# A recurrent attention cell behind two convolutions: its input product folded into the q, k and v weights, its convolutions on 32x32 tiles, its splits and stacks image by image

## The chip, the core and the metric

The kernel runs on one core of a Trainium2 chip. The core has TensorE (PE, matrix products; its weight loads are listed apart as PEld), VectorE (DVE), ScalarE (ACT), GpSimd (POOL) and SyncE (SP, which here only issues transfers). The engines run their own instruction streams in order and wait for each other by semaphores. The metric is the device time of one execution in microseconds.

## What is computed

Four layers follow each other on x of shape 4 x 32 x 32 x 32, each x + layer(gn(x)), where gn normalises every channel of every image: a second-order Volterra convolution (L0), a 3x3 convolution (L1), an attention cell (L2) and a Hartley transform layer (L3). The change is in L2, of which with a zero state only one attention of four has to be computed in full:

```python
xin = jnp.einsum('nchw,oc->nohw', x, W_in) + b_in[None, :, None, None]
h = jnp.zeros_like(xin)
pairs = ((xin, xin), (xin, h), (h, xin), (h, h))
for idx, (query, token) in enumerate(pairs):
    q = _conv(query, Wq[idx], 'SAME').reshape(n, HEADS, HC, -1)
    k = _conv(token, Wk[idx], 'VALID').reshape(n, HEADS, HC, -1)
    v = _conv(token, Wv[idx], 'VALID').reshape(n, HEADS, HC, -1)
    w = jax.nn.softmax(jnp.einsum('nhcq,nhcd->nhqd', q, k), axis=-1)
    a = jnp.einsum('nhcd,nhqd->nhcq', v, w).reshape(n, CA, hh, ww)
...
i, g, o = sigmoid(pre[0]), tanh(pre[2]), sigmoid(pre[3])
hout = o * jnp.tanh(i * g)
return jnp.einsum('nchw,oc->nohw', hout, W_out) + b_out[None, :, None, None]
```

There are 4 images of 4 heads of 8 channels, 1024 queries and 900 keys.

## The kernel before

All 4 images x 32 channels lie on the 128 partitions. The order of every engine's work is written out by hand. Line numbers are those of the profile.

L0 ends at L1007 and L1 runs from L1040 to L1060. Between the two PE multiplies zeros (`keep_clock`, L990), 3 + 4 + 13 times, until the second normalisation (DVE, L718) is there; then L1052 spreads the image over three row shifts. The third normalisation ends L1.

L2 then begins with the input product on PE (L1072, 24 products), added to its bias by ACT and DVE into a padded, three-fold copy `xst` (L631, L776). The convolutions for k, q and v follow (`conv`, L1084), each with 96 input rows (three row shifts of 32 channels) against 32 outputs. Between them stand three small products for the mean over the keys that the third attention needs (L1096, L1102, L1109). v is transposed by seven transposes and four products (L1115, L1120). k is split for all images at once into three bf16 parts (high, middle, low) and a difference of its two halves (`diff`), q likewise by halves of the image: ACT copies (L635 to L649), DVE subtracts (L793 to L822). SP writes each part to HBM (L508, L511) and reads it back three-fold, "stacked", into 72 rows (`stack_k` L519, `stack_q` L527), first two heads of k, then the q of image 0, then the rest of image 0 and 1.

The attention's order comes from `attention_plan` (L132). Half s is one half of an image's queries. For each of 16 groups of 128 queries PE makes two "max blocks" of 450 keys (L1137): a `diff` block, of which ACT takes the relu (L670), and a `first` block, to which DVE adds the relu and takes the maximum over keys (L870). I call them a pair. Blocks 0 to 31 are the 16 pairs of half 0. Then DVE splits the maxima (L847 to L854), PE turns them (item 32, L1149), DVE copies and POOL issues a transfer that puts them below the queries (L595). Blocks 33 to 45 belong to half 1. Then the first score tile comes (L1169), which ACT exponentiates (L662), and from there on scores, value products (L1187) and max blocks are woven together to the end of the last half. The PSUM bank of a block is taken from a ring of 7 banks for the first 41 items (`prologue`), then from a ring of 3, and PE waits until the bank's last block was read. After each of these first blocks PE multiplies zeros once, 256 columns.

## Time and profile before

| | us |
|---|---|
| median of 3 runs | 320.7 (318.45 to 322.28) |
| the profiled execution | 321.3 |
| its span, first to last instruction | 319.5 |
| PE busy | 291.6 |
| DVE busy | 209.0 |
| ACT busy | 183.5 |
| POOL busy | 30.2 |

The mean granted clock of TensorE was 0.994 of full speed. A busy PE means that a product was under way, not that the array was full. Times in the rows count from the start of the span; the profiled execution is 1.8 us longer than its span.

### The profile page before, as it was taken

What the parts mean: (1) busy time and instruction counts of PE and PEld (TensorE: products, weight loads), DVE (VectorE), ACT (ScalarE), POOL (GpSimd) and SP (SyncE); (2) the same over time, 40 slices, a digit from 0 to 9 for tenths busy, and PEclk for the clock granted to TensorE, in tenths of its full rate; (3) what the DMA queues carried; (4) which work ended last, traced back from release to release, by engine and by line L of the source; (5) the groups of instructions that cost most, each with busy time, mean ns of one, the idle gap of its engine ahead of it and who ended that gap; (6) DMA issues with size and microseconds to landing.
All of it is one profiled execution on the core that took longest, in us unless ns stands there. A gap on an engine that the chain in (4) does not pass through costs nothing.

```text
span 319.5 us, 10019 instructions
## 1 busy us (share of the span) xinstructions
PE 291.6 (91%) x4308; PEld 130.8 (41%) x4316; DVE 209.0 (65%) x483; ACT 183.5 (57%) x346; POOL 30.2 (9%) x34
## 2 busy tenths in 40 slices
PE   5999999798998999999999999999999899877774
PEld 2686634233455334333333333343333232334751
DVE  5980272577368647886977888879788122477664
ACT  1102011116246898897988888878888898313700
POOL 6400000010000000100100101001010010800000
PEclk9999999999999999999999999999999999999799
DMA  7100000003671483794000000000000000000001
GB/s 224 72 4 4 4 12 0 2 0 89 198 139 32 105 141 88 185 330 167 1 2 4 3 4 2 2 5 3 4 2 2 2 3 2 0 2 3 2 4 66
DMA packets 3819, 15.28 MB, mean 48 GB/s; under 512 B 807, under 2 KB 1623, under 8 KB 3359
## 3 DMA queue, kind: packets, MB, share of 16 engines
q1 hardware_dynamic: 3519, 14.54, 16.6%
q8 instruction: 34, 0.56, 0.8%
q0 software_dynamic: 256, 0.11, 0.2%
q14 instruction: 10, 0.08, 0.1%
HBM read 12.17 MB, written 2.37 MB: 45 GB/s over the span
## 4 chain that ended last, share of the span: by engine, by line
PE 41%; DVE 12%; issue 5%; ACT 5%; DMA 2%; ACTq 0%; DVEq 0%
PE ps L1187 11%; PE ps L1137 10%; PE ps L1169 10%; PE ps L1307 3%; ACT arena_b L662 3%; DVE sums L870 3%; DVE mx L875 3%; PE ps L1193 2%; PE ps L1252 2%; DMA arena_a<-mt_sb 2%; ACT arena_a L691 1%; PE ps L1328 1%; DVE arena_b L965 1%; DVE arena_a L940 1%; PE ps L1260 1%
## 5 line engine op out<-in xcount | busy, mean ns | idle before, releaser
L662 ACT ACTIVATE arena_b<-ps 128x512 f32<-128x512 f32 x232 | 126.3, 616 | 20.8 <-PE ps L1169 19.6
L1137 PE MATMUL ps<-arena_a 72*32 72x450 bf16 (+1 forms) x889 | 88.5, 355 | 3.0 <-DVE mx L870 1.5
L1169 PE MATMUL ps<-arena_a 75*32 75x512 bf16 x896 | 85.1, 380 | 0.8 <-DMA arena_a<-mt_sb 0.5
L875 DVE TENSOR_REDUCE mx<-ps 128x1 f32<-128x450 f32 x120 | 68.7, 618 | 3.6 <-PE ps L1137 3.5
L870 DVE CUSTOM_DVE_ANT_0 sums<-ps,relus 128x450 bf16<-128x450 f32 x68 | 42.1, 625 | 29.1 <-PE ps L1137 26.4
L1187 PE MATMUL ps<-arena_b,vt 128*32 128x512 f32 x448 | 58.9, 596 | 1.4 <-ACT arena_b L662 1.0
L1137 PEld LDWEIGHTS ps<-arena_a 72*32 72x32 bf16 (+1 forms) x889 | 27.6, 96 | 55.0 <-DVE mx L875 20.0
L990 PE MATMUL ps<-zeros 128*128 128x512 bf16 (+1 forms) x149 | 39.0, 370 | 5.7 <-DMA xa<-x 3.5
L670 ACT ACTIVATE relus<-ps 128x450 f32<-128x450 f32 x68 | 38.8, 570 | 9.4 <-PE ps L1137 8.1
L1169 PEld LDWEIGHTS ps<-arena_a 75*32 75x32 bf16 x896 | 24.9, 96 | 36.6 <-issue 14.1
L1019 PE MATMUL ps<-arena_a,cst 32*32 32x512 f32 x720 | 26.0, 609 | 0.0
L990 PEld LDWEIGHTS ps<-zeros 128*128 128x128 bf16 x157 | 15.1, 101 | 22.4 <-issue 9.5
L1019 PEld LDWEIGHTS ps<-arena_a,cst 32*32 32x32 f32 x720 | 17.9, 103 | 6.1 <-issue 1.7
L620 ACT ACTIVATE arena_b<-ps 128x512 f32<-128x512 f32 x6 | 3.1, 600 | 28.9 <-PE ps L1019 28.9
L1187 PEld LDWEIGHTS ps<-arena_b,vt 128*32 128x32 f32 x448 | 12.3, 109 | 9.8 <-ACT arena_b L662 4.7
L1084 PE MATMUL ps<-arena_b,cst 128*32 128x450 f32 (+1 forms) x144 | 15.8, 564 | 0.0
L691 ACT ACTIVATE arena_a<-arena_a 32x512 f32<-32x512 f32 x8 | 8.8, 1096 | 12.2 <-DVE arena_a L947 12.0
L732 DVE SCALAR_TENSOR_TENSOR arena_a<-xp 128x528 f32<-128x528 f32 (+6 forms) x24 | 15.2, 713 | 0.0
L595 POOL DMA_DIRECT2D arena_a<-mt_sb x8 | 5.2, 646 | 98.5 <-DVE mt_sb L884 98.5
L892 DVE STREAM_TRANSPOSE ot<-ps 128x512 f32<-128x512 f32 x8 | 5.7, 708 | 11.3 <-PE ps L1193 11.3
L602 POOL TENSOR_TENSOR on<-ot,rden 128x512 f32<-128x512 f32 x7 | 7.3, 1039 | 56.0 <-DVE rden L894 56.0
L1307 PE MATMUL ps<-arena_b,arena_a 128*64 128x64 f32 x256 | 9.2, 245 | 2.0 <-ACT arena_a L691 2.0
(130 smaller groups left out, 225.9 us busy)
## 6 DMA issues: line engine op xcount, KB each, us to landing
arena_b<-wmodes SPq DMA_DIRECT2D x1, 4096.0 KB, 20.5
arena_a<-k_scratch SPq DMA_DIRECT2D x9, 258.4 KB
arena_a<-q_scratch SPq DMA_DIRECT2D x12, 96.0 KB
arena_a<-q_scratch SPq DMA_DIRECT2D x3, 384.0 KB
k_scratch<-arena_b SPq DMA_DIRECT2D x3, 344.5 KB, 3.8
cst<-consts SPq DMA_DIRECT2D x1, 901.0 KB, 8.1
arena_a<-k_scratch SPq DMA_DIRECT2D x6, 129.2 KB
q_scratch<-arena_b SPq DMA_DIRECT2D x6, 128.0 KB, 5.0
```

Of the source, the lines that this page charges most:

```text
L662: nc.scalar.activation(probs[:, n % PRING, :], ps[:, SCORE_RING[n % len(SCORE_RING)], :], ACT.Exp).then_inc(expd, 1)
L670: nc.scalar.activation(relus[:, d % 3, :], ps[:, block_bank(i), 0:KHALF], ACT.Relu).then_inc(max_relu, 1)
L732: nc.vector.scalar_tensor_tensor(map_box(m, e), image_box(m, e), VOLTERRA_SCALE, image_box(m, e, *PRODUCTS[m]), ALU.mult, ALU.mult).then_i ...
L870: nc.vector.tensor_tensor_reduce(out=sums[:, d % 2, :], in0=bank, in1=relus[:, d % 3, :], scale=1.0, scalar=-3.0e38, op0=ALU.add, op1=ALU.max,
L875: nc.vector.tensor_reduce(mx[:, a, e:e + 1], bank, AX.X, ALU.max).then_inc(max_read, 1)
L990: mm(ps[:, bank, 0:cols], zeros[:, 0:P], zeros[:, 0:cols], start=True, stop=True)
L1019: last = mm(ps[32 * j:32 * j + 32, B * e + b, :].rearrange("p (y x) -> p y x", x=HALF_COLS), weights[rows], window(image[rows], py, px + e ...
L1084: last = mm(ps[32 * b:32 * b + 32, bank + e, 0:ny * cols].rearrange("p (y x) -> p y x", x=cols), weights[:, px, :], window(xst[:, b, :], f ...
L1137: last = mm(ps[j:j + width, block_bank(i), 0:KHALF], qst[0:PAIR_ROWS, e, g, qt * P + j:qt * P + j + width], kst[0:PAIR_ROWS, g, at:at + KH ...
L1169: last = mm(ps[32 * j:32 * j + 32, bank, :], kst[0:S_ROWS, g, k0:k0 + 32], qst[0:S_ROWS, e, g, :], start=True, stop=True)
L1187: last = mm(ps[32 * h:32 * h + 32, bank, :], vt[:, t, half % B * HEADS + h, :], probs[:, (n0 + h) % PRING, :], start=(t == 0), stop=False, ...
L1307: last = mm(banks(4 * l2, 4)[64 * jh:64 * jh + 64, 64 * k:64 * k + 64].rearrange("p (l o) -> p l o", l=2), xm[:, l2, jh, k, :], wv[:, ls, ...
```

## The change

W_in is multiplied into the 3x3 weights of q, k and v on PE (two products `wc` of 432 columns and nine of 96 for the bias, between L1 and its image shifts, with 11 instead of 20 products of zeros). The input product and its copies go. The convolutions read the normalised image directly, one tap after the other, each image on its own 32 rows and each kind of output on its own 32 columns of the array: `CONV_FIRST` makes q of the first half, both halves of k and their difference (156 products of at most 512 columns), `CONV_SECOND` v and q of the second half (120). The splits run by image, with q and k together; SP, ACT and POOL share the writes, ACT issues the reads of the first q. The zero columns of k are written to HBM at the start, the load of the row of ones for the maxima moves behind the first stacks. v is turned by 16 + 28 small products (`turn_values`) that stand between the max blocks, the three products for the mean stand there too (`means`), and ACT, no longer DVE, copies the turned v; POOL splits the q of the second half. The early max blocks use 3 banks, because conv results, v and the means hold the others.

```diff
+EARLY_RING = (0, 1, 2)
+SIDE_BANK = 3
...
+CONV_FIRST = (("q", 0), ("k", 0), ("k", 1), ("k", "diff"))
+CONV_SECOND = (("v", 0), ("v", 1), ("q", 1))
+TURNS_FIRST = 4
+TURNS_SECOND = 16
+MEANS_AT = (35, 39, 43)
...
-            ring = SCORE_RING + MAX_RING if i < prologue else MAX_RING
+            ring = EARLY_RING if i < early_blocks else MAX_RING
...
+            write_k(0)
+            write_k(1)
+            sp.wait_ge(kpad_written, 16)
+            sp.wait_ge(kd_written[0], 3 * 16)
             stack_k(0, 0, HEADS // 2)
...
             stack_k(1, HEADS // 2, HEADS)
+            sp.wait_ge(kd_written[1], 3 * 16)
             stack_k(2, HEADS, 2 * HEADS)
...
+                    if s == 0:
+                        pool.wait_ge(q1_copied, 1)
+                        nc.gpsimd.tensor_copy(q1_parts[:, :, 0, :], q1_raw).then_inc(q1_split, 1)
...
+            act.wait_ge(conv_done, 1)
+            high(0)
+            high(1)
+            middle(0)
+            middle(1)
+            act.wait_ge(split_l, 1)
+            act.dma_start(q_dram[0, :, :, 0:HEADS, :].rearrange("c t h n -> h c t n"), parts[0:32, 0]
+                          ).then_inc(qd_written[0], 16)
+            for b in (2, 3):
+                high(b)
+                middle(b)
+            act.wait_ge(qd_written[0], 16)
+            for s in range(PARTS):
...
+                act.dma_start(qst[r0:r0 + PARTS * HC, 0, 0:HEADS, :].rearrange("p g n -> p (g n)"),
...
+            nc.scalar.activation(vsb[0:32, :, 0:KHALF], ps[0:32, 4:8, 0:KHALF], ACT.Copy).then_inc(vsb_act, 1)
...
+                    if d == 8:
+                        act.wait_ge(vt_done, 1)
...
+                    elif d == ROWS_OF_MAX:
+                        act.wait_ge(vt_done, 2)
...
+                        nc.scalar.activation(q1_raw, ps[64:96, 4:8, :], ACT.Copy).then_inc(q1_copied, 1)
...
+            for i in range(2):
+                last = mm(ps[:, 5 + i, 0:432], c_("win4", 0, 32), qkvw[:, 432 * i:432 * i + 432], start=True, stop=True)
...
-            keep_clock(6, 13)
+            keep_clock(2, 11)
             pe.wait_ge(padded, 2)
...
+            def turn_values(job):
+                kind, t, b = job
+                if kind == "tile":
+                    at = (t % 4) * P + 32 * b
+                    return mm(ps[:, SIDE_BANK, at:at + 32], vsb[0:64, b, t * P:(t + 1) * P], c_("sumsel", 0, 64),
+                              start=True, stop=True)
...
+                if i < early_blocks:
+                    keep_clock(block_bank(i), 1, 256)
...
+            pe.wait_ge(split_r, B)
+            keep_clock(0, 2)
             pe.wait_ge(k_in[0], PARTS * 16)
+            keep_clock(0, 2)
             pe.wait_ge(q_in[0], PARTS * 16)
...
+                    if TURNS_FIRST <= i and first_turns:
...
+                        last = [turn_values(first_turns.pop(0)) for _ in range(2)][-1]
...
+                    elif TURNS_SECOND + 4 <= i and second_turns:
...
+                        last = [turn_values(second_turns.pop(0)) for _ in range(min(3, len(second_turns)))][-1]
...
+                    if i in MEANS_AT:
+                        means(MEANS_AT.index(i))
```

PE behind the third normalisation, before: the input product (L1072), the convolutions (L1084), the means (L1096, L1102, L1109), the turning of v (L1115, L1120) and zeros (L990) stand ahead of the first max block (L1137).

```order
L1072 MATMUL ps<-xp,cst 32x512 x24
L1084 MATMUL ps<-arena_b,cst 32x450 x24
L1096 MATMUL ps<-win,cst 128x9
L1084 MATMUL ps<-arena_b,cst 32x512 x24
L1102 MATMUL ps<-win,cst 32x1 x36
L1084 MATMUL ps<-arena_b,cst 32x450 x24
L1109 MATMUL ps<-a,cst 32x1 x12
L1115 MATMUL ps<-cst,arena_b 128x128 x7
L1120 MATMUL ps<-cst,arena_b 4x128 x4
L990 MATMUL ps<-zeros 128x512 x15
```

The same place now: behind the zeros (L1033) the first convolution's bias step (L1140) and its first tap (L1145); eight more taps like it follow, then the second convolution, and four products of zeros.

```order
L1033 MATMUL ps<-zeros 128x512 x10
L1140 MATMUL ps<-arena_a,on 32x512 x4
L1140 MATMUL ps<-arena_a,on 32x450 x8
L1145 MATMUL ps<-xp,on 32x512 x4
L1145 MATMUL ps<-xp,on 32x450 x8
L1145 MATMUL ps<-arena_b,on 32x450 x4
```

The small products have left this place, and the convolution starts straight from the normalised image.

PE at the first max blocks before, with what each waits for: stacks, then blocks (L1137) and zeros in turn.

```order
L990 MATMUL ps<-zeros 128x512 [waits k_in0]
L990 MATMUL ps<-zeros 128x512 x4
L1137 MATMUL ps<-arena_a 128x450 [waits vt_ready,q_in0]
L990 MATMUL ps<-zeros 128x256
L1137 MATMUL ps<-arena_a 128x450
```

The same place now, blocks 2 to 4 (L1201), each behind its zeros (L1033); L1157 is the turning of v.

```order
L1033 MATMUL ps<-zeros 128x256
L1201 MATMUL ps<-arena_a 128x450
L1033 MATMUL ps<-zeros 128x256 [waits max_relu]
L1201 MATMUL ps<-arena_a 128x450
L1033 MATMUL ps<-zeros 128x256 [waits max_read]
L1201 MATMUL ps<-arena_a 128x450
L1157 MATMUL ps<-cst,arena_b 128x32 [waits vsb_dve,vsb_act]
L1157 MATMUL ps<-cst,arena_b 128x32
```

From block 3 on, every block now waits for a read: an odd one for ACT's relu (max_relu), an even one for DVE's maximum (max_read).

ACT around the turn of the maxima before: the last copy of v (L651), relus (L670), then the first exponentials (L662).

```order
L651 ACTIVATE arena_b<-ps 128x900 [waits v_done]
L670 ACTIVATE relus<-ps 128x450 [waits max_scored] x3
L670 ACTIVATE relus<-ps 128x450 [waits max_read,max_scored] x20
L662 ACTIVATE arena_b<-ps 128x512 [waits scored] x2
L670 ACTIVATE relus<-ps 128x450 [waits max_read,max_scored]
```

The same place now, the relus at L710:

```order
L710 ACTIVATE relus<-ps 128x450 [waits max_scored] x3
L710 ACTIVATE relus<-ps 128x450 [waits max_read,max_scored] x6
L716 ACTIVATE vt<-ps 128x64x8 [waits vt_zeroed,vt_done]
L710 ACTIVATE relus<-ps 128x450 [waits max_read,max_scored] x8
L722 ACTIVATE vt<-ps 128x48x8 [waits vt_done]
L727 ACTIVATE vrest<-ps 4x4x8 x4
L731 ACTIVATE arena_b<-ps 32x2048
L710 ACTIVATE relus<-ps 128x450 [waits max_read,max_scored] x6
```

Seven copies now stand among the relus, six of them in one row between the relus of blocks 33 and 35.

## Rows read from the trace of the kernel before

**Rows 1.** Stages: length, busy time per engine (PE, PEld, DVE, ACT, POOL), clock, DMA share, GB/s.

```profile
60.40:91.05 30.65, 29.09 (x319) 12.05 (x321) 16.73 (x33) 9.27 (x14) 1.59 (x7) 1.00 0.36 91
...
107.70:271.50 163.80, 158.38 (x2309) 59.86 (x2308) 115.16 (x281) 142.26 (x282) 11.69 (x14) 1.00 0.19 51
```

**Rows 2.** Timeline of the early max blocks: start, length, engine, line, operation, [idle before].

```profile
91.05 0.35 PE L1137 MATMUL ps<-arena_a 72*128 72x450 bf16 x1
91.25 0.27 PE L990 MATMUL ps<-zeros 128*128 128x256 bf16 x1
91.36 0.35 PE L1137 MATMUL ps<-arena_a 72*128 72x450 bf16 x1
...
101.25 0.63 DVE L870 CUSTOM_DVE_ANT_0 sums<-ps,relus 128x450 bf16<-128x450 f32 x1
...
103.08 0.22 PE L1149 MATMUL ps<-ident_b,mparts 128*48 128x128 bf16 x1 [0.84 <-DVE mparts L854]
...
107.73 0.40 PE L1169 MATMUL ps<-arena_a 75*32 75x512 bf16 x4
```

**Rows 3.** Timeline of PE ahead of L1's image shifts.

```profile
43.03 4.26 PE L990 MATMUL ps<-zeros 128*128 128x512 bf16 x19
47.83 0.53 PE L1052 MATMUL ps<-xp,cst 128*32 128x386 f32 x3 [0.54 <-DVE xp L718]
```

**Rows 4.** Timeline of PE and PEld: the q convolution, the second mean, v's transposes.

```profile
73.26 5.36 PE L1084 MATMUL ps<-arena_b,cst 128*32 128x512 f32 x48
78.55 2.13 PE L1102 MATMUL ps<-win,cst 32*32 32x1 f32 x72
...
86.55 0.75 PEld L1115 LDWEIGHTS ps<-cst,arena_b 128*128 128x128 f32 x7 [0.65 <-ACT arena_b L651]
```

**Rows 5.** L0's products on 32x32 tiles (L1019) in one stretch: PE, PEld, clock.

```profile
32.00:36.00 4.00, 4.00 (x132) 2.32 (x104) 1.00 0.01 4
```

**Rows 6.** Groups by shape: count, then busy us, mean ns of one, idle before.

```profile
L647 ACT ACTIVATE arena_b<-ps 128x512 bf16<-128x512 f32 x2 | 1.2, 577 | 0.0
L815 DVE TENSOR_TENSOR arena_b<-ps,arena_b 128x512 f32<-128x512 f32 x2 | 1.4, 684 | 0.0
L649 ACT ACTIVATE arena_b<-arena_b 128x512 bf16<-128x512 f32 x2 | 1.3, 630 | 2.4 <-DVE arena_b L815 2.4
...
L635 ACT ACTIVATE arena_b<-ps 128x450 f32<-128x450 f32 x1 | 0.5, 545 | 4.8 <-PE ps L1084 4.8
L651 ACT ACTIVATE arena_b<-ps 128x900 f32<-128x900 f32 x1 | 0.9, 920 | 3.9 <-PE ps L1084 3.9
...
L1096 PEld LDWEIGHTS ps<-win,cst 128*128 128x128 f32 x2 | 0.3, 188 | 1.6 <-DVE win L788 1.6
...
L602 POOL TENSOR_TENSOR on<-ot,rden 128x512 f32<-128x512 f32 x7 | 7.3, 1039 | 56.0 <-DVE rden L894 56.0
```

**Rows 7.** Timeline of SP's transfers; then the stage in which the stacks arrive.

```profile
74.94 4.52 SPq L508 DMA_DIRECT2D k_scratch<-arena_b  x3
79.50 1.92 SPq L511 DMA_DIRECT2D q_scratch<-arena_b  x3
82.45 1.16 SPq L519 DMA_DIRECT2D arena_a<-k_scratch  x3
...
83.00:95.00 12.00, 11.25 (x107) 6.01 (x101) 5.04 (x18) 4.17 (x7) 0.69 (x5) 1.00 0.71 157
```

**Rows 8.** Timeline of blocks that wait for a bank in the ring of three.

```profile
106.13 0.63 DVE L870 CUSTOM_DVE_ANT_0 sums<-ps,relus 128x450 bf16<-128x450 f32 x1
...
106.82 0.11 PEld L1137 LDWEIGHTS ps<-arena_a 72*128 72x128 bf16 x2 [0.67 <-DVE mx L870]
...
107.22 0.55 ACT L670 ACTIVATE relus<-ps 128x450 f32<-128x450 f32 x1 [0.61 <-PE ps L1137]
...
107.90 0.63 DVE L870 CUSTOM_DVE_ANT_0 sums<-ps,relus 128x450 bf16<-128x450 f32 x1 [0.52 <-PE ps L1137]
```

**Rows 9.** A later stretch of PE: length, busy, clock.

```profile
298.00:302.00 4.00, 4.00 (x93) 0.59 0.02 4
```

More of the change, by code:

```diff
@@ L51 @@
 XPW = NP + 76
+XD_ROWS = 18
 EPS = 1e-5
@@ new lines, in means @@
+            def means(step):
+                images = [slice(32 * b, 32 * b + 32) for b in range(B)]
+                if step == 0:
+                    pe.wait_ge(vt_ready, 2 + HEADS)
+                    pe.wait_ge(win_ready, 6)
+                    mm(ps[:, SIDE_BANK, 16:25], c_("win"), win9[:, 0, :], start=True, stop=True).then_inc(win_done, 1)
+                elif step == 1:
+                    pe.wait_ge(win_scaled, 1)
+                    v2w = c_("v2w").rearrange("p (s o) -> p s o", o=32)
+                    for r in images:
+                        for s in range(9):
+                            last = mm(ps[r, SIDE_BANK, 0:1], v2w[r, s, :], win9[r, 1, s:s + 1], start=(s == 0), stop=(s == 8))
+                    last.then_inc(a2_done, 1)
+                else:
+                    pe.wait_ge(a2_ready, 1)
+                    proj2 = c_("proj2").rearrange("p (s o) -> p s o", o=32)
+                    for r in images:
+                        for i in range(3):
+                            last = mm(ps[r, SIDE_BANK, 8 + i:9 + i], proj2[r, i, :], a2[r, :], start=True, stop=True)
+                    last.then_inc(gb_done, 1)
@@ L1396, in layout_consts @@
     qkv = np.stack([np.asarray(i["L2_conv_" + n])[0] for n in ("Wq", "Wk", "Wv")])
-    put("qkv", qkv.transpose(3, 2, 0, 4, 1), 96)
+    put("win4", np.tile(np.asarray(i["L2_conv_W_in"]), (1, B)), 32)
+    put("qkvw", qkv.transpose(2, 0, 3, 4, 1), 32)
+    binbase = np.zeros((32, 8 + P), np.float32)
+    binbase[:, 8::32] = np.asarray(i["L2_conv_b_in"])[:, None]
+    put("binbase", binbase, 32)
+    qmask = np.zeros((B, 32, H, W), np.float32)
+    for u in range(3):
+        for v in range(3):
+            qmask[:, 3 * u + v, max(0, 1 - u):min(H, H + 1 - u), max(0, 1 - v):min(W, W + 1 - v)] = 1
+    put("qmask", qmask)
     put("v2w", np.tile(np.asarray(i["L2_conv_Wv"])[2].reshape(32, C, 9).transpose(1, 2, 0), (B, 1, 1)))
```

437 lines of the change are left out of this document (217 added, 220 removed).

## The prediction

> **What bounds the kernel now.** I read the stages first [rows 1], then the timeline of the stretch that the change rewrites, then the groups by shape for prices. From the first score (107.73) to 271.5 PE is busy 158.4 of 163.8 us: there a half follows the last without a gap, and the order of all engines in that stretch is the same in the changed kernel. So what the change does to the end is what it does to the time of the first score, one for one. That time is made of three pieces in the trace: the third normalisation, behind which L2 starts at 60.4; the first max block at 91.05 [rows 2]; and 16.7 us of early blocks up to 107.73. The first piece of 30.65 us is PE's too (29.09 busy). In the early blocks, the 16 pairs of half 0 take from 91.05 to 101.88, 10.8 us or 0.61 a pair beside the start; that is DVE's maximum of 0.63 at full speed, with seven banks to run ahead in. The turn ends at 103.30, and the 13 blocks behind it take 4.43.
>
> **L1's start.** PE gets two products of 432 columns and nine of 96 ahead of its zeros. A float32 product of 512 columns takes 0.89 (24 of them, four abreast, 5.36 us [rows 4]), so 432 take 0.75, two 1.5. The nine are limited by weight loads: two per product (48 records for 24 products), 0.75 / 7 = 0.107 each at 128 columns [rows 4], 18 of them 1.9 us. Nine zeros less save 9 x 4.26 / 20 = 1.9. The zeros started at 43.03 and left 0.54 idle [rows 3]; now they end at 43.03 + 1.5 + 1.9 + 2.35 = 48.8 where the image shifts began at 47.83: **1.0 us later** (0.4 if the nine run at their columns' pace, 2.5 at 0.19 a load, as the lone pair of L1096 took [rows 6]). L2 starts at 61.4.
>
> **The convolutions.** On 32x32 tiles L0 shows 132 records, 66 products, in 4 us: 0.061 each [rows 5]. The 156 products of the first convolution take 9.5 us, and the second, whose widest column has as many steps, the same: PE is through with them at 70.9 and 80.4. From this path go 96 products of the input and the convolutions, 11 of v's turning, 49 for the means and 15 of zeros. The difference image (one subtraction on DVE) is ready before its step comes.
>
> **Splits and stacks.** One image passes ACT 0.58, DVE 0.68, ACT 0.63, DVE about 0.69 [rows 6], with waits 2.9 us: the first is split at 73.9. ACT then splits images 2 and 3, alternating with DVE, until 78.9, and only then issues the three reads of the first q. SP issues two images' k, six transfers at some 0.65 (three of q took 1.92); the first image's are all issued at 75.9. Before, k's writes were issued by 79.46 and the reads behind them began at 82.45 [rows 7], so landing takes up to 3 us: stacks of k begin at 78.5 to 79. First k and first q are 3 x 132 and 3 x 98 KB (24 rows of 2 heads x 1378, or 4 x 512, in bf16), 690 KB, and the stage moved 157 GB/s: 4.4 us from 80, so the **first block stands at 84.4, 6.65 us earlier** than 91.05. It can hardly be earlier than 82.6: ACT's three issues (0.64 each, as SP's) and its copy of v (1800 columns, 1.67 us by the line through 545 ns at 450 and 920 at 900) come before its first relu. It is 86.9 if the next 400 KB of k share the engines fully.
>
> **Sixteen pairs in three banks.** Now block 2p waits for the maximum of pair p-2, and this pair's maximum for its own relu and block. Such a loop is in the trace [rows 8]: maximum 106.13, weight load 106.82, relu 107.22, next maximum 107.90: 1.77 us for two pairs. With zeros ahead of each block (256 columns, 0.11) it is 1.88, 0.94 a pair in place of 0.61. I stepped the recurrence through with those numbers; for before it gives 101.8 and 107.7, as measured. Sixteen pairs then last 16.0 with the copy of v's first part (0.6 on ACT): **5.2 us more**.
>
> **v's turning between the blocks.** A block with its zeros holds PE for 0.31 [rows 2]. Two turns add four loads of 0.107 and, as I count it, 0.1 for changing tile size twice: 0.84, against 0.47 that the ring allows a block. Eight blocks lose 0.37 each, 3.0. Four blocks with three turns (1.05) lose 2.3; six with three narrow ones (six records at 0.03, as the 72 of L1102, so 0.59) lose 0.7. That is 6.0; the recurrence, in which a little of it falls into ACT's copy, makes it **5.4 us**. Nothing else hides it: the ring leaves PE only 0.16 a block. If the turns ran at their columns' pace, this would be near 0; if every load were exposed at 0.19, 10.
>
> **Behind the turn.** After block 33's relu ACT makes six copies: 0.5, four of 0.2 and one of 2048 columns (1.87), 3.2 us, while every later relu waits behind them, and DVE and PE wait for those. PE's means product after block 35 also waits for them. Then the 5.5 pairs left take 5.2 at the ring's pace, and 36 mean products in their midst 2.13 [rows 4]. From the turn to the first score the recurrence gives 11.6 instead of 4.43: **7.2 us more**. Before, the same means stood on PE ahead of the first block; they are not saved but moved, and here DVE and ACT idle beside them.
>
> **What I cost at nothing.** POOL's split of the second q is four operations of 2048 columns, 4.2 us each by 1039 ns at 512 [rows 6]: 17 us that end about 21 us behind the turn. POOL's next transfer of maxima is due some 17 us after the first score, 28 behind the turn; beyond that cover it would cost us for us. The load of the ones moves behind SP's first stacks, but is wanted only at the first score.
>
> **Sum.** -6.65 + 5.2 + 5.4 + 7.2 = +11.1 us on the profiled execution's 321.3 gives 332.4; that execution is 0.6 above the median, so **332 us**.
>
> **A rule against the change.** A row first: the 32x32 products at 78.55 start 0.07 before the recorded end (78.62) of the products of another tile size [rows 4], and recorded ends trail the streaming by about 0.15 (91.05 + 0.35 against the next start at 91.25 [rows 2]). That is where my 0.1 comes from. The Trainium skill, "TensorEngine Tiling (Array Packing)", section Tiling Modes, says that changing the tiling mode drains TensorE. By a full emptying at both changes, 2 x 0.15 in place of 0.1 at 18 blocks, the sum grows by 3.6.
>
> **Rivals.**
> *The side work fits into the ring's waits (not slower).* Per pair PE works 0.62 and ACT 0.58 of 0.94; if turns, means and copies vanished in what is left, pairs cost 15.4, the turn 1.4, the other 6.5 pairs about 7: the first score at 108.2, **321 us**; 319 with the first block at 82.6. It decides where a pair with turns stays under 0.94. Against it: the turns are 9 us on nine pairs with 3 us of room, and the copies stand in one piece.
> *Each change of tile size empties the array in full.* As above: **335 us**. For it: each early block is now followed by other tiles. Against: 78.55.
> *The stacks come late and the clock falls.* PE has only 0.9 us of zeros for a wait of 4. Later in this trace, after PE stood for 2 us, 4 us ran at 0.59 of the clock [rows 9], between the levels of 2.4 and 1.2 GHz: 1.6 us lost. With the first block at 86.9 that is +4.1, **336 us**.
> *The ring doesn't pace and the side work is free (faster).* Then only the earlier block counts: 320.7 - 6.65 = **314 us**. It needs loops of 1.2 us; rows 8 show 1.77.
>
> **How the numbers follow.** The forecast has 0.63, the first rival 0.09, the emptying 0.15, the late stacks 0.10, the last 0.03. One per cent, 3.2 us, is about what a measurement of this kernel can tell from no change. So faster has 0.03, same 0.10 (the first rival and the near edge), slower 0.87. The range leaves out the first and the last rival: from 322 (turns nearly free and the first block at 82.6 put the first score at 111.5, which is 324 to 325, and less where the means find room) to 339 (both slower rivals together).
>
> **What would show it.** The first block (L1201) should stand near 84.4, PE idle for 3 us before it; pairs without turns at 0.94 and blocks with turns at 0.84 to 1.05 on PE; the sixteenth maximum at 105.8; a hole of about 3 us in ACT's relus after block 33, filled with copies; the first score (L1237) at 118.8, and the rest of the span as long as before. I am wrong if the first score comes before 111, or if the rest behind it grows or shrinks by over 2 us.

## The result and the profile after

| | before | after |
|---|---|---|
| median of 4 runs, us | 320.1 (318.5 to 322.3) | 366.5 (364.6 to 367.4) |
| profiled execution, its span | 321.3, 319.5 | 366.4, 364.6 |
| mean granted clock | 0.994 | 0.892 |

The ratio of after to before is 1.144, with a 95% interval of 1.135 to 1.152: 46 us slower, where 11 were forecast. The direction is right, the time lies far outside the range.

The stages of the changed kernel: busy time per engine (PE, PEld, DVE, ACT, POOL), granted clock, DMA share, GB/s.

```profile
44.00:51.00 7.00, 7.00 (x27) 4.00 (x26) 3.20 (x15) 1.03 (x3) 0.00 (x0) 0.54 0.00 1
64.00:69.00 5.00, 4.95 (x106) 2.51 (x121) 4.94 (x9) 0.00 (x0) 0.00 (x0) 0.66 0.01 3
...
86.40:96.10 9.70, 0.00 (x0) 0.00 (x1) 0.48 (x1) 0.89 (x1) 0.00 (x0) 0.63 0.77 167
97.10:134.40 37.30, 37.30 (x156) 20.73 (x154) 10.15 (x32) 9.22 (x17) 0.00 (x0) 0.50 0.20 39
134.40:151.40 17.00, 13.72 (x134) 7.44 (x132) 5.67 (x23) 6.58 (x13) 11.17 (x5) 0.60 0.51 102
151.40:161.00 9.60, 9.60 (x92) 4.18 (x96) 3.00 (x9) 6.80 (x14) 1.32 (x1) 0.52 0.30 93
161.00:315.00 154.00, 149.71 (x2204) 56.94 (x2192) 111.50 (x271) 133.38 (x263) 11.71 (x14) 1.00 0.11 38
```

The last row is the stretch of scores as in [rows 1], unchanged and at full clock. All that is new stands ahead of it. From 97.1 to 134.4, the 16 early pairs, PE is busy without a gap, and its clock is 0.50, the level of 1.2 GHz. In the kernel before the same 16 pairs had 1.00:

```profile
91.05:101.88 10.83, 10.78 (x70) 6.75 (x69) 9.71 (x32) 8.74 (x16) 0.00 (x0) 1.00 0.38 82
```

In the changed kernel the clock had already fallen while PE waited for k (0.63 over 86.4 to 96.1). Short stretches of half clock lie at L1's start (44 to 51), in the first convolution (64 to 69) and behind the first score (to 161).

PE's timeline at the places that the prediction named:

```profile
46.69 4.86 PE L1033 MATMUL ps<-zeros 128*128 128x512 bf16 x11
51.48 1.82 PE L1103 MATMUL ps<-xp,cst 128*32 128x386 f32 x15
...
96.10 1.25 PE L1033 MATMUL ps<-zeros 128*128 128x512 bf16 x3 [10.99 <-DMA arena_a<-k_scratch]
97.14 0.58 PE L1201 MATMUL ps<-arena_a 72*128 72x450 bf16 x1
...
106.27 0.58 PE L1201 MATMUL ps<-arena_a 72*128 72x450 bf16 x1
106.78 1.06 PE L1157 MATMUL ps<-cst,arena_b 64*128 64x32 f32 x4
107.77 0.40 PE L1033 MATMUL ps<-zeros 128*128 128x256 bf16 x1
107.96 0.58 PE L1201 MATMUL ps<-arena_a 72*128 72x450 bf16 x1
...
142.64 3.44 PE L1175 MATMUL ps<-win,cst 32*32 32x1 f32 x72
...
151.37 0.62 PE L1237 MATMUL ps<-arena_a 75*32 75x512 bf16 x4 [0.73 <-ACT relus L710]
```

L1's image shifts start at 51.48, not 47.83 [rows 3]: eleven zeros take 0.44 each, twice their time of before. The first block stands at 97.14 behind a wait of 11 us for k's stack. A block with two turns of v takes 107.96 - 106.27 = 1.69. The 72 products of the means take 3.44 where they took 2.13 [rows 4]. Against the steps of the prediction:

| step | forecast | measured |
|---|---|---|
| start of L2 | 61.4 | 64.05 |
| first convolution, to ACT's first split | 9.5 | 11.8 |
| split of the first image, to its first write | 3.0 | 2.7 |
| first write to first block | 10.5 | 18.5 |
| 16 pairs | 21.4 | 37.2 |
| 16th maximum to first score | 13.0 | 17.0 |
| first score to the end | 211.8 | 213.2 |

The differences sum to 34 us, which is what the forecast span of 330.6 lacks to 364.6. Two steps carry most of it: the pairs (16) and the way of k through HBM (8).

### The profile page after: what moved, and what is told of

Same layout as the page of the kernel before. It is cut to its first block, busy times and chain, and to the rows that moved or that the text cites. A ratio compares the mean times of both kernels' runs of the same rounds, so it can differ in the third digit from the quotient of the medians.

```text
span 364.6 us, 10910 instructions
## 1 busy us (share of the span) xinstructions
PE 327.3 (90%) x4756; PEld 157.7 (43%) x4756; DVE 206.2 (57%) x474; ACT 185.7 (51%) x351; POOL 42.7 (12%) x37
## 4 chain that ended last, share of the span: by engine, by line
PE 73%; DVE 11%; ACT 5%; issue 5%; DMA 5%; SPq 0%; ACTq 0%; DVEq 0%
PE ps L1201 15%; PE ps L1258 11%; PE ps L1237 10%; PE ps L1062 8%; PE ps L1033 8%; PE ps L1157 4%; PE ps L1145 3%; DMA arena_a<-k_scratch 2%; ACT arena_b L702 2%; PE ps L1391 2%; DVE sums L910 2%; DMA k_scratch<-arena_b 2%; PE ps L1264 2%; DVE mx L915 2%; PE ps L1336 1%
## 5 line engine op out<-in xcount | busy, mean ns | idle before, releaser
L1201 PE MATMUL ps<-arena_a 72*32 72x450 bf16 (+1 forms) x889 | 101.2, 375 | 2.1 <-DVE mx L910 1.0
L1237 PE MATMUL ps<-arena_a 75*32 75x512 bf16 x896 | 87.3, 391 | 0.9 <-ACT relus L710 0.7
L1033 PE MATMUL ps<-zeros 128*128 128x512 bf16 (+1 forms) x142 | 46.7, 433 | 17.0 <-DMA arena_a<-k_scratch 11.0
L710 ACT ACTIVATE relus<-ps 128x450 f32<-128x450 f32 x68 | 37.4, 552 | 48.0 <-PE ps L1201 47.9
L1201 PEld LDWEIGHTS ps<-arena_a 72*32 72x32 bf16 (+1 forms) x889 | 29.4, 99 | 52.0 <-DVE mx L915 21.0
L1237 PEld LDWEIGHTS ps<-arena_a 75*32 75x32 bf16 x896 | 25.5, 98 | 38.4 <-issue 16.9
L1033 PEld LDWEIGHTS ps<-zeros 128*128 128x128 bf16 x142 | 15.1, 113 | 39.6 <-issue 13.7
L1145 PE MATMUL ps<-xp,on 32*32 32x450 f32 (+1 forms) x432 | 19.7, 611 | 0.0
L1258 PEld LDWEIGHTS ps<-arena_b,vt 128*32 128x32 f32 x448 | 12.2, 110 | 10.2 <-ACT arena_b L702 4.8
L1145 PEld LDWEIGHTS ps<-xp,on 32*32 32x32 f32 x432 | 14.0, 106 | 4.4 <-issue 2.5
L1157 PEld LDWEIGHTS ps<-cst,arena_b 64*128 64x128 f32 x56 | 12.8, 321 | 6.8 <-issue 6.8
L1157 PE MATMUL ps<-cst,arena_b 64*128 64x32 f32 x56 | 14.4, 402 | 0.0
## 6 DMA issues: line engine op xcount, KB each, us to landing
arena_a<-consts SPq DMA_DIRECT2D x1, 1076.0 KB, 10.2
```

The lines of the kernel that those rows point to most:

```text
L710: nc.scalar.activation(relus[:, d % 3, :], ps[:, block_bank(i), 0:KHALF], ACT.Relu).then_inc(max_relu, 1)
L1033: mm(ps[:, bank, 0:cols], zeros[:, 0:P], zeros[:, 0:cols], start=True, stop=True)
L1145: last = mm(dst, wcomb[rows, KINDS[kind], step - 1, :], conv_rows(image, kind, e, u, v), start=(step == 1 and e == "diff"), stop=(step == ...
L1157: return mm(ps[:, SIDE_BANK, at:at + 32], vsb[0:64, b, t * P:(t + 1) * P], c_("sumsel", 0, 64), start=True, stop=True)
L1201: last = mm(ps[j:j + width, block_bank(i), 0:KHALF], qst[0:PAIR_ROWS, e, g, qt * P + j:qt * P + j + width], kst[0:PAIR_ROWS, g, at:at + KH ...
L1237: last = mm(ps[32 * j:32 * j + 32, bank, :], kst[0:S_ROWS, g, k0:k0 + 32], qst[0:S_ROWS, e, g, :], start=True, stop=True)
```

## The experiments

Every profile gives the same four stages, in us (from the start of L2 to the first block, 16 pairs, to the first score, the rest):

| run | time | L2 to block | 16 pairs | to score | rest |
|---|---|---|---|---|---|
| before | 320.1 | 30.6 | 10.8 | 5.9 | 211.8 |
| after | 366.5 | 33.1 | 37.2 | 17.0 | 213.2 |
| e1 zeros in the wait | 361.4 | 30.6 | 35.4 | 17.0 | 212.9 |
| e13 as e1, no turning | 341.4 | 31.4 | 15.9 | 16.1 | 212.5 |
| e6 as e1, zeros behind turns | 358.6 | 31.8 | 34.7 | 16.9 | 212.9 |
| e5 as e1, six banks | 356.7 | 32.5 | 31.9 | 11.4 | 214.3 |
| e2 side work in the wait | 351.0 | 42.2 | 16.3 | 8.1 | 219.0 |
| e4 as e2, seven banks | 341.5 | 44.3 | 11.0 | 5.7 | 214.8 |
| e3 before, three banks | 332.2 | 30.6 | 14.8 | 7.8 | 216.9 |
| e7 L1 and order of k | 366.6 | 26.8 | 37.2 | 17.1 | 215.5 |
| e9 one write, small bias | 364.1 | 32.6 | 37.3 | 16.8 | 213.1 |
| e11 k's scratch by rows | 360.5 | 28.1 | 37.2 | 15.8 | 213.0 |
| e8 v by transposes | 331.2 | 29.0 | 10.8 | 6.7 | 214.0 |
| e10 repairs, one write | 333.5 | 32.2 | 12.1 | 7.1 | 220.5 |
| e12 repairs, rows | 321.2 | - | - | - | - |
| e14 as e12, stack alone | 323.5 | 29.4 | 10.8 | 5.7 | 212.2 |

The times of e10, e12 and e14 are medians of 4, 11 and 10 executions, those of the other experiments are of one execution each. Executions of one kernel lie 3 to 5 us apart (before 318.5 to 322.3, e10 330.5 to 334.7), so the argument goes by the stages more than by the times. The dashes are explained at e12.

### The clock in the early pairs

Three theories: the wait of 11 us drops the clock (A); the early stretch itself does, by its ring of three or by v's turning (B, later split into R and T); the clock is a bystander (C).

**e1: zeros in the wait.**

```diff
             pe.wait_ge(split_r, B)
-            keep_clock(0, 2)
+            keep_clock(0, 50)
             pe.wait_ge(k_in[0], PARTS * 16)
```

> The changed kernel, with 50 products of zeros (10.65 us at 0.213) instead of 2 while PE waits for the first k. Theory A (the clock falls to half because PE idles for 11 us before the first block, and the rest follows): the granted clock is 1.00 at the first block (97.1), the 16 pairs with their turns then take the 21.4 us of my working instead of 37.2, and turn to first score 13 instead of 17; first score about 131, time 345 to 348. Theory B (the early blocks in a ring of three, with turns and means between them, are themselves too sparse for the full clock): the clock starts at 1.00 and falls again within the pairs; at most 5 us gained, 361 to 366. Theory C (the clock has no part in it, the blocks wait for banks and weight loads): clock 1.00 and still 37 us for the pairs, 366.

It took 361.4: B's number. PE at the first two turns of this run, then the stage behind them:

```profile
96.05 0.35 PE L1201 MATMUL ps<-arena_a 72*128 72x450 bf16 x1
96.33 0.63 PE L1157 MATMUL ps<-cst,arena_b 64*128 64x32 f32 x4
96.89 0.28 PE L1033 MATMUL ps<-zeros 128*128 128x256 bf16 x1
97.01 0.35 PE L1201 MATMUL ps<-arena_a 72*128 72x450 bf16 x1
97.30 0.63 PE L1157 MATMUL ps<-cst,arena_b 64*128 64x32 f32 x4
97.86 0.40 PE L1033 MATMUL ps<-zeros 128*128 128x256 bf16 x1
98.05 0.58 PE L1201 MATMUL ps<-arena_a 72*128 72x450 bf16 x1
```

```profile
98.00:129.50 31.50, 31.28 (x134) 17.40 (x134) 8.22 (x28) 7.59 (x14) 0.00 (x0) 0.50 0.16 35
```

The clock is full through the wait and the first blocks. At 97.86, 1.5 us behind the first turn, the zeros grow from 0.28 to 0.40 and the block from 0.35 to 0.58, and so it stays for 31 us. At full clock the block with two turns took 97.01 - 96.05 = 0.96, at half 1.69. A falls: the wait costs the pairs 1.8 us (37.2 - 35.4), and the turns bring the clock down without it.

**e13: no turning.** The largest term by itself:

```diff
-                        last = [turn_values(first_turns.pop(0)) for _ in range(2)][-1]
+                        first_turns = first_turns[2:]
                         if not first_turns:
-                            last.then_inc(vt_done, 1)
+                            mm(ps[:, SIDE_BANK, :], zeros[:, 0:P], zeros[:], start=True, stop=True).then_inc(vt_done, 1)
```

(and the same for the second turns).

> Run e1 (50 products of zeros in the wait) without the 44 products that turn v: two products of zeros stand where their results are signalled, so v's tiles hold zeros and the output is not the reference's. Ring of three, copies and means as changed. Compared with e1 (34.8 us from the first block to the 16th maximum, 17.7 from there to the first score). If the turning drops the clock: 1.00 through the pairs, 0.94 a pair, 15 to 16.5 us for the 16; then 13 to 15 to the first score; time 338 to 342. If the ring of three drops it without the turning: 1.18 a pair, 18.5 to 19.5, and 17 to 18 behind it, time 345 to 347.

It took 341.4, within what the turning's theory said. Its 16 pairs:

```profile
94.90:110.80 15.90, 13.41 (x70) 5.24 (x69) 10.00 (x32) 9.13 (x17) 0.00 (x0) 1.00 0.40 83
```

Full clock, 15.9 us, and that with PE idle for 2.5 of them, while the changed kernel's PE, busy for all of its 37.3, had half clock. So between these two runs the 44 products of v cost 35.4 - 15.9 = 19.5 us. The ring of three alone doesn't drop the clock here. Behind the pairs, among the copies and the means, the clock fell in this run too (0.50 from 115 to 135), and the way to the first score took 16.1, not the 13 to 15 expected.

**e6: zeros behind the turns.** e1 and

```diff
                     keep_clock(block_bank(i), 1, 256)
+                    if TURNS_FIRST < i <= TURNS_FIRST + 8 or TURNS_SECOND + 4 < i <= TURNS_SECOND + 8:
+                        keep_clock(block_bank(i), 2)
```

> As the first run, with two more products of zeros of 512 columns in each of the 12 blocks that follow a block with 128-wide turns (12 x 2 x 0.213 = 5.1 us at full clock, 10.3 at half). Theory T (sparse turns drop the clock, dense zeros can hold it): clock 1.00 or nearly, the 16 pairs 26 to 30 us instead of 35, time 352 to 357. If the clock's fall has another reason than what PE streams there: 0.50 as before, 10 us more, 370 to 372.

```profile
94.50:105.50 11.00, 10.95 (x64) 6.62 (x65) 2.73 (x10) 2.19 (x4) 0.00 (x0) 1.00 0.37 82
112.00:127.00 15.00, 14.78 (x73) 6.93 (x74) 3.08 (x9) 2.73 (x5) 0.00 (x0) 0.50 0.01 2
```

Both numbers missed: 34.7 us and 358.6. Through the eight blocks with two turns the clock stayed up with the zeros, at 1.39 a block, 0.43 of it zeros: 0.96 again for the block itself. Among the blocks with three turns it fell after all. The first of them was still at full clock:

```profile
109.31 0.35 PE L1203 MATMUL ps<-arena_a 72*128 72x450 bf16 x1
109.60 0.85 PE L1157 MATMUL ps<-cst,arena_b 64*128 64x32 f32 x6
110.38 0.50 PE L1033 MATMUL ps<-zeros 128*128 128x256 bf16 x2
110.93 0.35 PE L1203 MATMUL ps<-arena_a 72*128 72x450 bf16 x1
```

It took 1.62, 1.19 without its 0.43 of zeros. In the pairs the zeros gained 0.7 us over e1: holding the clock with them paid for itself and little more. The 2.8 us between the two times had come by the start of L2 (60.6 for 63.5), where the code is the same.

**e5: six banks.** e1, with the copy of the second q moved into ACT's wait:

```diff
-EARLY_RING = (0, 1, 2)
+EARLY_RING = (0, 1, 2, 7, 4, 5)
```

> As the first run (50 products of zeros in the wait, turns and means between the blocks), but ACT copies the second q in the wait already, so the early blocks have six banks instead of three and their zeros a bank of their own. Compared with the first run (361.4). Theory T (the turns' small float32 products drop the clock by themselves): 0.50 from some 2 us behind the first turn on, 1.69 us for a block with two turns as there, 30 to 33 us for the 16 pairs, first score 138 to 143, time 353 to 359. Theory R (only turns together with the ring's waits leave PE sparse enough): clock 1.00, blocks with two turns 0.95, the 16 pairs about 20 us, first score 122 to 126, time 336 to 341.

T again: 31.9 us for the pairs, first score at 140.5, 356.7. Only the fall came later than T had it, at 104, some 5 us behind the first turn and not 2. The shorter way to the first score (11.4) comes of the copy of q that no longer stands there and of the wider ring, which this run doesn't tell apart.

**e2 and e4: the side work in PE's wait.** All turns, the means and ACT's copies stand before the first block, in banks 1, 2 and 3; e4 then has the banks (0, 1, 2, 7, 3, 4, 5).

```diff
+            means(0)
...
+            [turn_values(job) for job in first_turns][-1].then_inc(vt_done, 1)
+            means(1)
...
+            [turn_values(job) for job in second_turns][-1].then_inc(vt_done, 1)
+            means(2)
...
             pe.wait_ge(k_in[0], PARTS * 16)
```

> The changed kernel with the turning of v, the means and ACT's copies of v and q moved out of the early blocks into PE's wait for the first k (other banks, 10 products of zeros among them); ring of three as changed. The moved work is about 44 x 0.21 + 3 us, and may push the first block from 97.1 to about 100 or 101. Theory A (idle wait drops the clock): PE is busy through the wait, clock 1.00 at the first block, pairs at 0.94, sixteenth maximum 15 to 16 us behind the first block, first score about 125, time 339 to 342. Theory B (the ring of three is too sparse by itself): the clock is at or falls to 0.50 in the pairs, 1.18 a pair, first score about 130, time 344 to 347. Theory D (the turns between the blocks are the cost, clock or not): pairs lose about 0.5 us against the changed kernel wherever a turn stood, which by itself is 18 us off the pairs.

> As the second run, and the early blocks take seven banks again, which the moved copies set free; zeros between the blocks go to a bank of their own, as in the kernel before. First block about 100 to 101 as there. Theory A and B both: clock 1.00, 0.61 to 0.67 a pair, 11 us for 16 pairs, 6 to 7 from the last maximum to the first score; first score about 118, time 331 to 333. If the clock stays at half for other reasons: 0.9 to 1.2 a pair, first score 125 or later, time over 339. If banks were never the limit: as the second run.

e2 by stages:

```profile
88.00:105.80 17.80, 17.13 (x178) 14.98 (x179) 0.53 (x4) 1.72 (x6) 0.00 (x0) 0.50 0.60 118
108.00:130.00 22.00, 17.48 (x89) 6.65 (x88) 14.35 (x48) 11.59 (x22) 5.91 (x3) 1.00 0.16 37
132.00:142.00 10.00, 10.00 (x90) 3.07 (x88) 3.17 (x10) 7.05 (x16) 4.68 (x2) 0.50 0.66 126
```

The small products took the half clock with them to where they now stand: 17 us in place of the 12 allowed, so the first block came at 105.8 and both times are above what was expected (351.0 and 341.5). Without them the ring of three took 16.3 us for its pairs, at full clock from 108 on. Seven banks then gave 11.0 and 5.7, the kernel before's numbers. Between these two runs the four more banks are worth 5.2 in the pairs and 2.4 to the score. The rest differs by 4.2: in e2 the clock fell for ten us in the middle of busy scores.

**e3: three banks in the kernel before.**

```diff
-            ring = SCORE_RING + MAX_RING if i < prologue else MAX_RING
+            ring = (0, 1, 2) if i < early_blocks else MAX_RING
```

> The kernel before with three banks instead of seven for its early blocks, nothing else. My recurrence: 0.94 a pair without the zeros in the bank's way 0.89, so the 16 pairs take 14.3 to 15.5 instead of 10.8 and the blocks behind the turn 2 us more; first score 113 to 115, time 326 to 328, with the clock at 1.00. Theory B (a ring of three is too sparse for the full clock): the clock falls within the early blocks, 1.18 a pair, first score about 118 to 120, time 331 to 334. The rival that the ring doesn't pace: 320 to 321.

```profile
90.20:112.60 22.40, 17.75 (x92) 6.71 (x91) 14.74 (x50) 12.58 (x23) 0.76 (x1) 1.00 0.25 58
112.70:125.50 12.80, 12.78 (x112) 5.19 (x116) 3.81 (x12) 8.21 (x16) 0.00 (x0) 0.50 0.75 133
```

The first score at 112.7 is 5 us late, at full clock, about as the recurrence had it. The time, 332.2, is not: the clock fell just as the scores began, and 5 us more were lost there. Neither theory had that.

### L1's start and the way of k

**e7.** Two edits:

```diff
                           start=(tap_ == 0), stop=(tap_ == 8))
+                keep_clock(4, 1)
             last.then_inc(wc_done, 1)
-            keep_clock(2, 11)
...
             write_k(0)
-            write_k(1)
             sp.wait_ge(kd_written[0], 3 * 16)
             stack_k(0, 0, HEADS // 2)
+            write_k(1)
```

> The changed kernel with two edits read in two places. (1) Nine of the eleven zeros ahead of L1's image shifts stand between the nine bias products, two go. Theory T: the clock stays at 1.00 there, image shifts at 48.8 to 49.2 instead of 51.5. If the fall at 44 to 51 doesn't come from the row of small products: 0.50 as before, shifts at 50.5 to 51. (2) SP reads the first stack of k before it writes the second image's k. If the wait for the first block (11 us) is made of the transfers queued ahead, the wait shrinks by about 5; if it is made of the DMA engines' share, by 1 to 2. Behind the first block nothing is changed (half clock as now). Time 357 to 360 with both, 363 to 365 with neither.

The first edit failed: half clock lasted from 46 to 57, the shifts came at 54.2. Zeros between small products didn't hold the clock here. From L2 to the first block 6.2 us were saved. 1.6 of them are a convolution at full clock (10.2 to ACT's first split, 11.8 in the changed kernel), 4.6 the second edit's, but not where they were expected: the read of the first stack began 7.8 us behind the first write, as in the changed kernel; from there to the first block it took 6.1 instead of 10.7.

```profile
81.04 2.30 SPq L533 DMA_DIRECT2D k_scratch<-arena_b  x3
88.84 1.25 SPq L541 DMA_DIRECT2D arena_a<-k_scratch  x3
...
93.87 1.25 PE L1033 MATMUL ps<-zeros 128*128 128x512 bf16 x3 [6.36 <-DMA arena_a<-k_scratch]
```

The sum, 366.6, hides both.

**e9.** Bias products on 32 rows, and one write per image:

```diff
-                last = mm(ps[:, 3, 0:96].rearrange("p (a o) -> p a o", a=3), c_("binbase", 0, 32)[:, 8 - tap_:8 - tap_ + P],
+                last = mm(ps[0:32, 3, 0:96].rearrange("p (a o) -> p a o", a=3), c_("binbase", 0, 32)[:, 8 - tap_:40 - tap_],
...
+                sp.dma_start(k_dram[b, :, :, :, 0:3 * KHALF].rearrange("h c t (j n) -> j (h c) t n", j=3),
+                             parts[32:128, b, :, 0:KHALF]).then_inc(kd_written[b], 16)
```

> The changed kernel with two edits read in two places. (1) The nine bias products are taken on 32 output rows instead of 128 (and copied to the four blocks by ACT), so that their 18 loads have 32 columns instead of 128, about 0.04 instead of 0.17 us. If these loads cause the clock's fall at 44 to 51: 1.00 there, image shifts at 47.2 to 48.2 instead of 51.5. If not: 50 or later. (2) k of an image goes to HBM in one transfer from 96 partitions instead of three from 32. If 32 partitions keep only a quarter of the DMA engines busy (share 0.26, 50 to 118 GB/s in the run before): landing 3 to 5 us behind the first issue instead of 8, first block 25 to 27 us behind the start of the convolutions instead of 33. If the landing is a fixed latency: 31 to 33. Behind the first block nothing is changed: 54 us to the first score. Time 354 to 358 with both, 366 with neither.

The shifts came at 50.0, with half clock for 3 us of the zeros. That is no proof for the bias: with the changed kernel's code there, the other runs have 50.9 to 51.7, but e6 has 48.0. The single write was worse: its data landed 11.9 us behind its issue, with 96 partitions. So too few partitions isn't it.

**e11.** Head and channel as one dimension in k's scratch, and the order of e7:

```diff
-        k_dram = nc.dram_tensor("k_scratch", [HC, PARTS, G, KW], BF16, kind="Internal").ap()
+        k_dram = nc.dram_tensor("k_scratch", [B, HEADS, HC, PARTS, KW], BF16, kind="Internal").ap()
...
+                    sp.dma_start(k_dram[b, :, :, :, (j - 1) * KHALF:j * KHALF].rearrange("h c t n -> (h c) t n"),
+                                 parts[32 * j:32 * j + 32, b, :, 0:KHALF]).then_inc(kd_written[b], 16)
```

> The changed kernel with k's scratch in HBM laid out so that head and channel are one dimension of 32 rows (the read of a stack keeps its rows of 2.7 KB), and SP reading the first stack before it writes the second image's k, as in e7. In the kernel before a write of k had 16 rows of heads in its slowest dimension and moved at a DMA share of 0.6 to 0.9; in the changed kernel it has 4 (heads of an image) and moves at 0.25, in e9 and e10 it had 3 (kinds) and took 12 us. If the slowest dimension decides how many DMA engines take part: share over 0.5 in the writes, the three writes land at most 3 us behind their last issue (before: 5.3), first block 23 to 25.5 us behind the start of the convolutions, against 33.1 as changed and 26.8 with the order alone. If it doesn't: 26 to 28. Behind the first block as now, 54 us to the first score. Time 355 to 359 with it, 359 to 362 without.

While the first writes run, in four kernels (the DMA share is the number before the last). Before, 128 partitions to 16 groups of rows:

```profile
76.00:79.00 3.00, 3.00 (x42) 0.98 (x31) 2.58 (x5) 1.55 (x4) 0.00 (x0) 1.00 0.73 174
```

After, 32 partitions to 4 heads:

```profile
80.00:83.00 3.00, 3.00 (x101) 2.55 (x91) 1.54 (x3) 1.71 (x3) 0.41 (x1) 1.00 0.27 69
```

e10, whose single write is that of e9, 96 partitions to 3 kinds (q's writes beside it, 32 to 4, as in the others):

```profile
76.00:80.00 4.00, 4.00 (x121) 3.05 (x99) 1.98 (x3) 2.30 (x4) 1.66 (x2) 1.00 0.26 61
```

e11, 32 partitions to 32 rows:

```profile
80.00:83.00 3.00, 3.00 (x98) 2.30 (x80) 1.23 (x2) 1.71 (x3) 0.76 (x1) 1.00 0.59 129
```

A quarter of the engines' time at the factors 4 and 3, over half of it at 32: the write's outermost dimension sets it. The Trainium skill, "DMA: Bandwidth & Descriptors", section "Why a DMA increments its semaphore by 16 and not by 1", states the rule: a transfer runs on the largest number of engines up to 16 that divides the slowest dimension of both its sides. By that it is 16, 4, 3 and 16 here, and the traces agree: in their DMA records each of these writes has as many packets of 4 bytes at its end, 16, 4, 3 and 16. The read of the stack now began 5.6 us behind the first write instead of 7.8. The first block came 28.1 us behind the start of L2, though, not 23 to 25.5, and not before e7's 26.8: the convolution ran at half clock for some us (66 to 69), and from the stack's issue to the first block it took 8.0. The time, 360.5, lies where it was expected without the gain.

### Putting it together

**e8.** The edits of e7, seven banks, and v by transposes: copies out of PSUM put it on 128 partitions.

```diff
+            for b in range(B):
+                nc.scalar.activation(vs[32 * b:32 * b + 32, 0:KHALF], ps[0:32, 4 + b, 0:KHALF], ACT.Copy)
...
+                for t in range(DT):
+                    last = nc.tensor.transpose(ps[:, SIDE_BANK if t < 4 else SIDE_BANK2, (t % 4) * P:(t % 4 + 1) * P],
+                                               vs[:, t * P:(t + 1) * P], c_("ident"))
```

> The two edits of the run before, and v brought onto 128 partitions by its copies out of PSUM, then turned by 7 transposes and 4 products as in the kernel before, with the means and the copies, in the wait for the first k; ring of seven with zeros in a bank of their own. Folded weights, 32x32 convolutions and splits by image stay. Theory T with the ring: the clock is 1.00 throughout, first block 88 to 91, 16.8 us from there to the first score as in the kernel before and in the fourth run, so first score 105 to 108 and 317 to 321. If transposes and means drop the clock too: 0.50 from about 86, 6 to 10 us more. If the stacks still come as late as now: first block 94, time 325.

```profile
114.00:115.30 1.30, 0.06 (x5) 0.07 (x8) 0.76 (x4) 0.55 (x1) 1.30 (x1) 1.00 0.02 4
117.00:126.00 9.00, 9.00 (x80) 3.37 (x76) 3.17 (x10) 6.60 (x14) 6.16 (x3) 0.50 0.79 149
```

35 us better than the changed kernel, 331.2, and some 10 above the forecast. 8 of them had come by the start of L2 at 68.8, since L1's start had lost the clock as in e7; the stacks were late, and the first score waited 1.3 us with PE idle and was followed by nine us of half clock.

**e10.** e8 without the zeros of e7, with both edits of e9.

> Run e8 without its interleaved zeros, and with the two edits of e9: folded weights, 32x32 convolutions and splits by image stay as changed, v is turned by transposes in the wait, ring of seven, k written in one transfer per image. If the explanation is complete (small loads in a row drop the clock; three banks and side work between the blocks stretch the early stretch; small transfers are slow): clock 1.00 throughout, convolutions from 60.5 to 61.5, first block 23 to 25 us later at 84 to 87, first score 16.7 to 17.5 behind it at 101 to 104, 212 us from there to the end, time 315 to 319, ratio to the kernel before 0.985 to 0.995. If a part is missing (the clock falls behind the first score again, or the stacks come late): 322 to 330.

It missed: 333.5, ratio 1.042 (1.035 to 1.048). L2's start at 60.2 was near the forecast, but the single write landed 12.5 us behind its issue, so that the first block stood at 92.4. The first score came 19.3 behind it, not 16.7 to 17.5, and the rest grew to 220.5, with half clock at 112 to 119 and 130 to 140.

**e12.** e10 with k's scratch as in e11; ACT and DVE share the copy of the second q, and 16 fewer products of zeros stand in PE's wait.

> Run e10 with k's scratch as in e11 instead of the one write from 96 partitions, and the copy of the second q shared by ACT and DVE. Folded weights, 32x32 convolutions and splits by image as changed. If the explanation is complete: convolutions from 60 to 61.5, first block 25 to 27 us later at 86 to 88, first score 16.7 to 17.5 behind it at 103 to 105.5, 212 to 213 from there to the end, clock 1.00 but for some us; time 317 to 321, ratio 0.99 to 1.005. If the clock falls behind the first score again, as in e8 and e10, or the stacks of the later images come late: 323 to 330.

321.2 us, ratio 1.004 (0.999 to 1.009): level with the kernel before, 45 us below the changed one. Ten of its eleven executions lie between 320.0 and 324.5. The eleventh, which is the one profiled, took 333.8, and its stages are left out of the table. Its early pairs:

```profile
91.40:113.20 21.80, 21.80 (x74) 10.51 (x72) 11.15 (x38) 8.75 (x16) 0.00 (x0) 0.50 0.34 78
```

The clock had fallen at 86, ahead of a wait for k, and stayed at half through blocks and zeros with no small products among them. Why it didn't rise there stays open.

**e14.** e12, four more products of zeros in PE's wait, and

```diff
             write_k(1)
+            sp.wait_ge(k_in[0], PARTS * 16)
             stack_k(1, HEADS // 2, HEADS)
```

> Run e12 with SP waiting for the first stack of k to land before it issues the second and third, and four more zeros in PE's wait. If the first stack was slow because of the transfers issued behind it: 5 to 6 us from its issue to the first block (8 to 10 in e11 and e12), first block 3 us earlier at 86 to 88, first score 103 to 106, time 317 to 319. If the stack is slow by itself: as e12, 321; if the later stacks then come late and PE waits for them in the ninth pair: 322 to 325.

```profile
89.70:106.20 16.50, 15.36 (x97) 9.25 (x96) 13.97 (x49) 12.20 (x23) 3.60 (x3) 1.00 0.57 131
106.20:270.00 163.80, 157.00 (x2296) 59.71 (x2300) 115.16 (x281) 140.87 (x278) 20.67 (x17) 1.00 0.19 51
```

SP's transfers in the same run:

```profile
74.89 2.40 SPq L533 DMA_DIRECT2D k_scratch<-arena_b  x3
80.78 1.76 SPq L541 DMA_DIRECT2D arena_a<-k_scratch  x3
82.58 2.33 SPq L533 DMA_DIRECT2D k_scratch<-arena_b  x3
88.99 2.37 SPq L541 DMA_DIRECT2D arena_a<-k_scratch  x6
```

Its profiled execution (320.2, the shortest of ten) has the early blocks of the kernel before and the first score at 106.3, 1.4 us earlier than before. The median is 323.5, ratio 1.008 (1.003 to 1.013): holding back the other stacks gains nothing. The first stack, issued at 80.78, landed at 88.99: 8.2 us with nothing of SP's behind it but the second image's write. It is not slow by itself, though. The same bytes took 9.6 in the changed kernel and 5.0 in e7, and in the kernel before they landed at 86.34, 3.9 behind the issue at 82.45 [rows 7], by the trace's records of semaphore updates, which tell when a transfer is complete. These runs differ in the transfers beside the stack and in the length of its rows, and what sets the time stays open. No version beat the kernel before.

## Why the prediction was wrong

**What bounds it: right.** From the first score on, the kernel is the one of before; all but 1.4 us of the loss lies ahead of it. That loss is a sum of stages, as forecast; the first block alone has the wrong sign.

**Sixteen pairs in three banks: right.** The loop of 16.0 us for 16 pairs took 15.9 (e13), the rival that the ring doesn't pace was wrong, and so was the rival that the side work fits in its waits.

**v's turning: the step that failed.** Forecast 5.4, measured 35.4 - 15.9 = 19.5 (e1 and e13), and 1.8 more in the changed kernel, where the clock had fallen in the wait before them. The mechanism, PE's time between the blocks, was right, and its price at full clock nearly so: 0.96 a block with two turns for my 0.84. What I left out is that the price was taken at a clock that the turns don't keep. At half clock that block took 1.69, and a block without turns 0.59 for 0.31. An estimate of the split: 8 blocks at 0.96, 0.12 over mine, and 4 blocks with three turns at 1.19 (e6), 0.14 over mine, make the turning about 6.9 at full clock; the other 13 are the clock. I did have the clock as a rival, but as something that a wait brings on and that heals in 4 us, because [rows 9] was the only such row. e1 removed the wait and gained 5 us, of which 1.8 in the pairs; e13 removed the small products and gained 20 more. The changed kernel without its turns, but with its wait, was not run; e12's profiled execution shows that half clock can outlast a wait by 22 us without them.

**L1's start: right but for the clock.** Forecast 1.0 late, measured 3.65. Where the clock stayed up in a run with the same code (e6), the 18 loads took 2.14 us for my 1.9, and the shifts came at 48.0, 0.2 late. In the changed kernel they took 3.1, and the zeros behind them 4.9 instead of 2.35.

**The convolutions: short by 2.3.** 10.3 at full clock (e8) for my 9.5, and 11.8 with five us at 0.66: 0.8 is the size, 1.5 the clock.

**Splits and stacks: the second step that failed.** 10.5 us from the first write to the first block were forecast, 18.5 measured. I let the writes land in 3 us, as those of [rows 7] did; the first image's took 5.3 behind their last issue, because an image has 4 heads where all four had 16 (e11). With 32 rows they took 3.5 (e11). And I took 4.4 for the stacks from a mean of 157 GB/s; in the changed kernel, with three stacks issued behind one another, it was 10.7 from the read's issue to the first block, 9.6 of it until k landed. The rows of the kernel before don't hold that time: from 82.45 [rows 7] to 91.05 [rows 2] are 8.6 us, but PE was busy with v's transposes and zeros and met no wait for a transfer:

```profile
86.58 0.96 PE L1115 MATMUL ps<-cst,arena_b 128*128 128x128 f32 x7 [0.59 <-DVE gb L828]
87.47 0.40 PE L1120 MATMUL ps<-cst,arena_b 128*4 128x128 f32 x8
88.03 3.19 PE L990 MATMUL ps<-zeros 128*128 128x512 bf16 x14 [0.16 <-issue]
91.05 0.35 PE L1137 MATMUL ps<-arena_a 72*128 72x450 bf16 x1
```

By the semaphore updates the first k had landed there at 86.34 and the first q at 90.0: 7.5 us for what the mean rate gives 4.4.

**Behind the turn: size off by 4.** 17.0 for 13.0. The copies took 3.2 as forecast; the means 3.44 for 2.13, and the blocks about them ran at half clock. Moving the copy of q away, with six banks, gave 5.6 us (e5).

**The rest: +1.4**, ten us of half clock behind the first score. POOL's split was hidden, as costed.

**The emptying at a change of tile size** was not told apart: 0.96 is 0.12 over my price, where the rival's full emptying asks for 0.2, and no run here isolates it.

## What to carry to other kernels

When work is cut into small products, take their price from rows in which such products run for as long as they will, and look at the granted clock there, not at the busy share: a PE that is busy all the time can be at half speed. When a transfer is cut into smaller ones, look at what its outermost dimension becomes, and take its time from issue to landing in a like place rather than from a mean rate or from the first use, which other work can hold up. Work moved out of a serial stage into a pipelined one needs the pipeline's slack, in banks and in time, and here it took both.

## What the runs showed that was not expected

- Full clock with PE idle for 2.5 of 15.9 us (e13), half clock with PE busy for 37.3 of 37.3 (after).
- The clock can fall behind the stretch that seems to bring it on: in e3 it stayed up for 22 us in the ring of three and fell when the scores began, for 13 us with PE busy. Why there, stays open.
- Products of zeros between small products held it through eight blocks in e6 and not in e7.
- The same code does not always lose the clock: L1's start, unchanged, lost it in the changed kernel and in six experiments, and kept it in e6.
- Half clock can outlast what brought it: 22 us of blocks and zeros, PE busy throughout, in e12's profiled execution.
- One write from 96 partitions (253 KB) landed after 12 us, three from 32 (84 KB each) after 7.8, and the same three with 32 rows on the far side after 5.6.
